# One step of an order moved: the first expert's output products behind the first third of the second expert's

## What is computed

```
scores = softmax(x @ gate_w.T);  topk_w, topk_idx = top_k(scores, 6);  topk_w /= topk_w.sum()
buf[e, c] = the rows sent to expert e (at most C = 768 of them)
g = einsum('ecd,efd->ecf', buf, w_gate);  u = einsum('ecd,efd->ecf', buf, w_up)     # 64 experts, f = 176
eo = einsum('ecf,edf->ecd', silu(g) * u, w_down)
y[row] += eo[e, c] * weight;   out = layernorm(x + y + shared_swiglu(x))
```

## Time and profile before

| | us |
|---|---|
| median of three runs | 2341.12 |
| the profiled execution, whole | 2346.05 |
| its span, first to last instruction | 2344.2 |
| TensorE busy in the span | 2204.0 (94%) |
| GpSimd busy in the span | 818.0 (35%) |

### The profile page before, as it was taken

One profiled execution on the slowest core, in us unless ns is written; L12 is line 12 of the kernel. 1 busy time (PEld: TensorE's weight loads), 2 busy tenths in 40 slices (PEclk: granted clock), 3 DMA queues, 4 the chain that ended last, 5 costly groups with the idle time before them and its releaser, 6 DMA issues.

```text
span 2344.2 us, 38656 instructions
## 1 busy us (share of the span) xinstructions
PE 2204.0 (94%) x14773; PEld 1987.1 (85%) x14776; DVE 1328.2 (57%) x2870; ACT 1201.9 (51%) x2231; POOL 818.0 (35%) x791
## 2 busy tenths in 40 slices
PE   8999999999999999999999999988888999999970
PEld 7999998998989899898889889877777888888860
DVE  4444444545555454555545455647657888878753
ACT  4544444444444454444444444434435777777753
POOL 3111112000024400002530000360445888888785
PEclk9999999999999999999999999999899999999995
DMA  5766722221113212211421211241548988888856
GB/s 197 314 271 263 272 80 62 57 71 59 50 58 120 83 59 77 60 43 63 147 65 47 91 43 44 67 138 49 197 147 267 213 202 212 195 212 199 211 63 230
DMA packets 152704, 310.60 MB, mean 132 GB/s; under 512 B 26528, under 2 KB 88224, under 8 KB 152512
## 3 DMA queue, kind: packets, MB, share of 16 engines
q1 hardware_dynamic: 103888, 251.98, 32.1%
q0 software_dynamic: 48192, 55.68, 12.3%
q10 hardware_dynamic: 432, 0.40, 0.1%
HBM read 168.01 MB, written 149.34 MB: 135 GB/s over the span
## 4 chain that ended last, share of the span: by engine, by line
PE 83%; DVE 7%; issue 4%; ACT 3%; DMA 2%; POOL 2%; another core or an unknown queue 1%; SPq 0%; ACTq 0%; POOLq 0%; DVEq 0%
PE bank L852 51%; PE bank L1212 19%; PE bank L862 7%; PE bank L1315 2%; PE bank L1225 2%; DVE ub L1717 1%; POOL y_part L2116 1%; ACT q_hi L1440 0%; DVE stats L2031 0%; DVE bank L1901 0%; DMA xr<-slots 0%; POOL slots L2106 0%; DVE yn L1739 0%; ACT silu_b L1516 0%
## 5 line engine op out<-in xcount | busy, mean ns | idle before, releaser
L1212 PEld LDWEIGHTS bank<-v,a 128*128 128x128 f32 x4608 | 604.8, 191 | 44.5 <-ACT a L1464 0.8
L1212 PE MATMUL bank<-v,a 128*128 128x129 f32 x4608 | 618.1, 275 | 0.8 <-ACT a L1464 0.6
L2116 POOL DMA_INDIRECT y_part<-y_e,row_token x264 | 413.9, 1568 | 104.1 <-issue 82.4
L2086 POOL TENSOR_TENSOR decay_all<-decay_all,tab 128x128 f32<-128x128 f32 x128 | 61.6, 481 | 945.0 <-DMA decay_all<-decay_dram 944.7
L1460 ACT ACTIVATE a<-bank,c_s 128x512 f32<-128x512 f32 x384 | 263.2, 687 | 182.2 <-PE bank L852 164.4
L1464 ACT ACTIVATE a<-ub 128x512 f32<-128x512 f32 (+1 forms) x256 | 134.0, 524 | 381.9 <-DVE ub L1717 357.3
L2106 POOL DMA_INDIRECT slots<-rows,slot_u x192 | 189.4, 986 | 291.5 <-PE bank L1212 124.6
L852 PE MATMUL bank<-q_hi,k_hi 128*128 128x512 f32 (+1 forms) x640 | 262.7, 410 | 10.8 <-DVE ub L1717 9.5
L1696 DVE TENSOR_TENSOR q_lo<-bank,q_hi 128x512 fp32r<-128x512 f32 x128 | 88.5, 692 | 282.0 <-ACT q_hi L1440 273.5
L852 PE MATMUL bank<-q_lo,k_hi 128*128 128x512 f32 (+1 forms) x640 | 238.1, 372 | 0.0
L852 PE MATMUL bank<-q_hi,k_lo 128*128 128x512 f32 (+1 forms) x640 | 237.2, 371 | 0.0
(11 more groups left out here) (215 smaller groups left out, 4909.1 us busy)
## 6 DMA issues: line engine op xcount, KB each, us to landing
slots<-acc SPq DMA_DIRECT2D x65, 816.0 KB, 7.8
w_raw_f<-in_wffn SPq DMA_DIRECT2D x66, 624.0 KB
xr<-slots SPq DMA_DIRECT2D x64, 544.0 KB
decay_all<-decay_dram SPq DMA_DIRECT2D x128, 128.0 KB
w_hi<-w_dram SPq DMA_DIRECT2D x24, 384.0 KB, 3.9
w_lo<-w_dram SPq DMA_DIRECT2D x24, 384.0 KB, 4.5
sum<-y_part SPq DMA_DIRECT2D x16, 512.0 KB, 10.5
wc_hi<-wc_dram SPq DMA_DIRECT2D x24, 256.0 KB, 2.7
```

Of the source, the lines that this page charges most:

```text
L1212: ins = e.matmul(dst[:, tt, r, :], a32[u % NA][:, r, t0:t0 + P], v[n % 3][:, s, :], start=(s == 0 and r == 0), stop=(s == 2 * g + tt), ski ...
L2086: e.tensor_tensor(arg[:, GROUP:GROUP + P], arg[:, P:GROUP], mask, ALU.add)
L2116: e.indirect_dma_start(out=y_part[part], out_offset=bass.IndirectOffsetOnAxis(ap=token, axis=0), in_=y_e[y][:, j, :], in_offset=None, boun ...
```

## The change

At place 1, the second expert, both pairs of `down` of the first expert move up in the list. They stood behind part 2 of the second expert's products and behind its `hidden` parts 2 and 3; they now stand behind part 0 of its products, the turning of the third expert's rows and the split of a weight. At all other places the order is as it was.

```diff
             turn(after[0])
         if len(after) > 1:
             do("split_hi", after[1])
+        if place == 1:
+
+            down(SEQ[0], (0, 1))
         do("gate_up", k, 1)
...
         do("gate_up", k, 2)
         do("hidden", k, 2)
-        if place:
+        if place > 1:
             down(SEQ[place - 1], (0,))
         do("hidden", k, 3)
         if len(after) > 1:
             do("split_lo", after[1], 2)
-        if place:
+        if place > 1:
             down(SEQ[place - 1], (1,))
```

## The result

| | before | after |
|---|---|---|
| median of 22 runs each, run in turn | 2341.33 us | 2346.14 us |
| profiled execution: time, span | 2346.05, 2344.2 us | 2349.49, 2347.6 us |
| mean granted clock of its span | 0.978 | 0.976 |

The ratio of the changed kernel to the one before is 1.0023, with a 95% interval of 1.0013 to 1.0033. On 2341.33 us that is 5.4 us slower, 3.0 to 7.7. The forecast was 3.7 slower with a range to 2347.5, and rival A 5.0 and more. The time lies in the range, but on rival A's side of the forecast, and a little beyond the 0.2% within which I gave 0.70. The two medians themselves differ by 4.8 us.

The account below looks back on a forecast made before the run. It took the DVE and ACT loop to bound until about 1825 us, then PE, and POOL at the end. Steps 1 to 4 (2.5 us) plus the clock (1.2) made 3.7 on 2341.12: 2344.8 us, range 2341.0 to 2347.5.

Parts of the forecast that it names:

- rival A: Clock stays low over most products behind the wait at place 1: 5.0 us slower or near 6, 2346.1 to 2347; chance 0.27.
- signs of being wrong: PE's idle stretch doesn't grow, POOL's last add isn't later, or the clock stays low past 1792.
- Step 1: PE at place 1: `down` starts unmoved at 1785.90, twelve products come after it; third expert's part 0 is 2.75 us later.
- the unknown: `silu_a` at 1783.95 waited 1.61 us for PE; with timely notice `down` could start near 1782, PE losing 2.1 to 2.4.
- Steps 2 and 3: DVE and ACT, second expert: multiply 2.65 us late, `silu_b` 2.85; after what comes back, the loop is some 2.5 late.
- Step 4: DVE and ACT's loop to 1825 has no slack; POOL takes the shift to the end; steps 1 to 4 sum to 2.5 us.
- rival C: First expert's outputs reach POOL 1.5 us earlier and POOL, ending last, keeps that: faster, 2339.6 us; chance 0.05.
- Rival B: Wait is hidden: the loop from 1787 to 1825 has slack and POOL's queue absorbs the rest, 2341.1 to 2342; chance 0.10.
- Step 5: PE's idle before `down` grows from 3.15 to 5.9 us and the clock may fall: 1.2 us, bounds 0 to 2.5.

Follow-up runs that it names:

- e10: Changed kernel with first expert's `down` still further ahead, before the third expert's rows are turned into the bank; 2348.62 us, ratio 1.0015 to the kernel before.
- e9: Changed kernel with the last three parts of the overflow-job table made at places 22, 26, 30 instead of 3, 4, 5; 2342.55 us, ratio 0.9987.
- e1: Changed kernel with PE repeating the twelve products of parts 1 and 2 while it waits before the moved `down`; 2344.05 us, ratio 1.0007.
- e4: Kernel before with only PE's products of `down` moved as in the change, ACT's `y_e` left in place; 2346.9 us, ratio 1.0010.
- e3: Kernel before with twelve extra products directly behind `down` of the first expert at place 1; 2340.79 us, ratio 0.9989.
- e7: Changed kernel with the move of `down` made at every place instead of place 1 alone; 2511.68 us, ratio 1.0713 to the kernel before.
- e11: Kernel before with POOL's twelve fetches for the overflow jobs issued at place 8 instead of place 0; 2352.94 us, ratio 1.0037.
- e5: Kernel before with only ACT's `y_e` (and POOL's adds) moved as in the change, PE's products left in place; 2343.56 us, ratio 0.9997.
- e6: Kernel before with first expert's `down` moved behind part 1 of the second expert's products, so only part 2 leaves the wait; 2342.92 us, ratio 1.0007.
- e8: Kernel before with the last three parts of the overflow-job table made at places 22, 26, 30 instead of 3, 4, 5; 2338.91 us, ratio 0.9974.

## Why the prediction was right, and what of it was off

None of the signs of being wrong appeared: PE's idle stretch grew, the clock was back before 1792, and POOL's last add came later (534.04 behind the anchor, 530.85 before). The mechanism held; the size of one term did not.

**Step 1, PE.** The reading that the bank and not the operands holds `down` is shown by e10. The idle was foreseen as 5.9 us, as `down` would start unmoved 18.1 behind the anchor. It was 4.50, with `down` 16.05 behind the anchor; in e9 it was 6.11, with `down` 18.03 behind. In all kernels that leave the fetches alone `down` starts 15.3 to 18.1 behind the anchor, whether it was moved or not (moved 15.3 to 18.1, not moved 16.7 to 18.1). I take that as the late notice varying, as the paragraph on the unknown allowed; with one profile of each kernel it isn't shown that the move has no part in it.

**Steps 2 and 3.** Foreseen 2.5 us for the products behind the wait, net of what comes back; measured 2.6 by e1, with the reserve said there. ACT's order gives back 0.5 to 0.65 in it (e4), foreseen 0.72. The third expert's turning lost its wait of 0.64 as stated.

**Step 4, what carries it.** The delay reached POOL at the fifth expert and stayed: right in the outcome. My reason, the loop of DVE and ACT without slack, is only half of it: e9 took that loop's load away and the price was the same. The idle of 4.94 us of POOL, the engine that ends last, is enough. Its earlier first add (0.5 us from `down`, 2.6 from the anchor, foreseen 1.5) was worth nothing, so rival C is refuted. The reading that POOL idles just 0.30 from 1832.27 on was too simple: in the kernel before it also waited up to 3.6 us at a time there, so its queue is not full throughout. Rival B is refuted by the stretches and by e9; only e3 speaks for it.

**Step 5, the clock.** This is the term that was mis-sized: I took 1.2 and it was 2.0 (e1), within its bounds of 0 to 2.5. Its form was right, a low stretch of 6.8 us that began 1.7 ahead of `down`: it began at 1783.5, 1.9 ahead. I took half the price because of doubt whether it would fall at all; it fell in the profile after, in e4, e9 and e10 and with four gaps of e7, and these eight are the gaps over 4.2 us before a `down`. So the doubt was misplaced. The local sum is 2.6 + 2.0 = 4.6 instead of 3.7, and the whole kernel lost 5.4 (3.0 to 7.7), which also leaves out the 2.6 counted from the anchor. Rival A charged the clock in full and was nearer by its 5.0. The Trainium skill, in "TensorE: Matmul & The Clock Gate", section "Why this matters for your kernels", warns against gaps between bursts of matmuls; taken strictly, it gave 5.0 here. The long gaps here, 4.28 to 7.43 us, bear it out. The gaps of 3.15, 3.18 and 3.21 us, which kept the full clock, don't, and in e7 the fall came even with gaps of 1.9 us, in 24 of 52.

**Still open.** Why TensorE's notices come late while the overflow fetches run; e11 ties the one to the other, not how. Why e3's delay doesn't show in its time. And how the irregular waits of POOL after 1830 us come about, and whether they make the 20 us between executions; between the profiles of two kernels that stretch differed by up to 7 us.

## What to carry to other kernels

Work that fits in a wait which another engine ends is free. Moving the waiting work ahead of it doesn't end the wait sooner: it puts the filler on the path, and the emptied gap may cost the clock for the burst behind it; price that in full when the gap becomes clearly longer than any that kept the clock, and don't count on the full clock because a gap is short, above all when it comes back at every step. Ask what the engine that ends last gains: an earlier first piece is worth nothing to it if it then runs dry before the second. To see 0.2% in a profile, measure from a common event near the change to the last point where the bounding engine still waits, try a second such event, and take more than one profile where the two disagree; the medians only confirm the sign.

## What the hardware showed that I had not expected

- A product's end can be noticed late by other engines. In the kernel before, `silu_a` started at 1783.95 for a product that had ended near 1777.2, 6.7 us, with the DMA share at 1.01 and POOL's fetches in flight; without those fetches (e11), at the same DMA share, it started at 1777.42, as soon as ACT was free, and PE's wait of 3.15 us was 0.31.
- The clock isn't told by the length of the last gap alone: it fell with 3.10 us of idle (e5) and 2.42 (e3), and stayed with 3.15 (before), 3.18 (e6) and 3.21 (e8). With gaps of 1.9 us at nearly every place (e7) it was low in 24 of 52 `down`s.
- Twenty products of 256 columns took 2.46 us in the kernel before and 4.40 at the granted clock of 0.50, nearly the full factor between the two levels.
